# Four transformer stages on one core: the weight fold on column tiles, keys parked in fetch order, late weights as steps of ScalarE, the low-rank product on two row tiles

## What is computed

```python
x = layernorm(x + attn0(x))   # 16 heads of 8, causal; q and k are low rank: x @ a @ b
x = layernorm(x + ffn0(x))    # silu(x w1) * (x w2), gelu(h1), gelu(h2), w3; width 512
x = layernorm(x + attn1(x))   # 16 heads of 8, not causal, softmax / sqrt(128)
x = layernorm(x + ffn1(x))    # below

# ffn1: the token's best expert of 8 picks a low-rank term of rank 4
top1 = argmax(x @ gate.T + gate_b)
h    = relu(x @ wi.T + wi_b + (x @ A[top1].T) @ B[top1].T)
out  = h @ wo.T + wo_b
```

## Time and profile before

| | us |
|---|---|
| median of 3 runs | 928.54 (925.82 to 929.03) |
| the profiled execution | 927.51 |
| its span, first to last instruction | 925.70 |
| PE busy | 870.4 (94%) |
| DVE busy | 670.8 (72%) |
| ACT busy | 488.5 (53%) |
| POOL busy | 185.6 (20%) |
| DMA, mean over the span | 70 GB/s |

### The profile page before, as it was taken

One profiled execution on the slowest core, in us unless ns is written; L12 is line 12 of the kernel. 1 busy time (PEld: TensorE's weight loads), 2 busy tenths in 40 slices (PEclk: granted clock), 3 DMA queues, 4 the chain that ended last, 5 costly groups with the idle time before them and its releaser, 6 DMA issues.

```text
span 925.7 us, 19247 instructions
## 1 busy us (share of the span) xinstructions
PE 870.4 (94%) x7076; PEld 689.3 (74%) x7076; DVE 670.8 (72%) x2379; ACT 488.5 (53%) x951; POOL 185.6 (20%) x389
## 2 busy tenths in 40 slices
PE   5589899999999999999999999999999999999996
PEld 4358687876777876688777887778867888787855
DVE  5767658749998579964799659965899659654863
ACT  1143454376655545645547665646565665562372
POOL 2132221003400233002320034002320114010211
PEclk9879899999999999999999999999999999999999
DMA  7613031402322034301252023400442022002200
GB/s 243 205 47 104 20 98 53 126 13 60 105 71 77 1 93 129 87 2 37 68 145 76 2 70 113 116 10 1 118 115 71 7 75 65 13 8 63 81 15 12
DMA packets 49044, 65.17 MB, mean 70 GB/s; under 512 B 5624, under 2 KB 42744, under 8 KB 44248
## 3 DMA queue, kind: packets, MB, share of 16 engines
q1 hardware_dynamic: 46552, 58.02, 21.9%
q10 hardware_dynamic: 2400, 5.93, 1.9%
HBM read 48.46 MB, written 14.68 MB: 68 GB/s over the span
## 4 chain that ended last, share of the span: by engine, by line
PE 65%; DVE 12%; DMA 11%; issue 4%; ACT 4%; SPq 3%; POOL 1%; ACTq 0%; POOLq 0%; DVEq 0%
PE banks L1003 19%; PE banks L916 8%; PE banks L934 8%; DMA krow<-scratch 7%; PE banks L883 6%; PE banks L985 5%; PE banks L1052 4%; DVE top L704 3%; PE banks L838 2%; DMA scratch<-split 2%; DMA qrow<-tsplit 2%; SPq L439 1%; PE banks L874 1%; PE banks L1033 1%; PE banks L1034 1%
## 5 line engine op out<-in xcount | busy, mean ns | idle before, releaser
L575 ACT ACTIVATE prob<-banks 128x384 f32<-128x384 f32 (+1 forms) x512 | 247.0, 550 | 117.2 <-PE banks L916 97.4
L704 DVE TENSOR_REDUCE top<-banks 128x2 f32<-128x512 f32 (+1 forms) x280 | 176.0, 680 | 38.5 <-PE banks L883 27.9
L695 DVE CUSTOM_DVE_ANT_0 banks<-banks,above 128x128 f32<-128x128 f32 x448 | 145.5, 388 | 42.0 <-PE banks L883 29.6
L916 PE MATMUL banks<-qrow,krow 75*128 75x256 bf16 (+1 forms) x1024 | 155.6, 266 | 8.6 <-ACT prob L575 3.9
L883 PE MATMUL banks<-krow,qrow 72*128 72x256 bf16 x768 | 133.9, 277 | 9.2 <-DVE top L704 5.0
L916 PEld LDWEIGHTS banks<-qrow,krow 75*128 75x128 bf16 x1024 | 89.5, 100 | 47.0 <-ACT prob L575 11.2
L934 PE MATMUL banks<-prob,v 128*32 128x256 f32 (+1 forms) x2048 | 122.8, 367 | 0.7 <-POOL prob L515 0.6
L508 POOL TENSOR_TENSOR ln_rstd<-ln_var,minus_half 128x2 f32<-128x2 f32 x64 | 44.8, 703 | 380.6 <-DVE ln_var L764 380.3
L1003 PE MATMUL banks<-glu,wh 128*128 128x256 f32 x512 | 116.5, 381 | 1.0 <-ACT prob L575 1.0
L1003 PE MATMUL banks<-hid,wh 128*128 128x256 f32 x512 | 115.9, 380 | 0.0
L1003 PEld LDWEIGHTS banks<-glu,wh 128*128 128x128 f32 x512 | 94.9, 190 | 13.8 <-ACT prob L575 1.2
(11 more groups left out here) (100 smaller groups left out, 1164.1 us busy)
## 6 DMA issues: line engine op xcount, KB each, us to landing
qrow<-scratch SPq DMA_DIRECT2D x30, 576.0 KB
krow<-scratch SPq DMA_DIRECT2D x90, 192.0 KB
scratch<-split SPq DMA_DIRECT2D x96, 128.0 KB, 1.9
xt<-in_xt SPq DMA_DIRECT2D x16, 128.0 KB, 2.4
x<-in_x SPq DMA_DIRECT2D x16, 128.0 KB, 2.7
wh<-in_wh ACTq DMA_DIRECT2D x2, 1024.0 KB, 8.5
out<-xout SPq DMA_DIRECT2D x16, 128.0 KB, 2.0
qrow<-tsplit SPq DMA_DIRECT2D x90, 8.0 KB
```

Of the source, the lines that this page charges most:

```text
L575: nc.scalar.activation(prob[s][:, j % 2, g, 0:wide], banks[:, b, 0:wide], ACT.Exp, scale=1.0 / float(np.sqrt(np.float32(HD))) if s == A0 e ...
L695: done = nc.vector.tensor_tensor_reduce(out=bank[:, g * wide:(g + 1) * wide], in0=bank[:, g * wide:(g + 1) * wide], in1=above[:, 2 * P - w ...
L704: nc.vector.tensor_reduce(out=dst, in_=src, axis=AX, op=ALU.max, negate=True).then_inc(maxed[s], 1)
L916: done = nc.tensor.matmul(bank[:, kb * SEQ:(kb + 1) * SEQ - q0], krow[s][n % DEEP[s]][0:ROWSM, h, kb * P:(kb + 1) * P], qrow[s][n % DEEP[s ...
```

## The change

**The fold.** The factors change roles: 16 products with 16 columns of weights (`wqb`) and 128 moving columns (`wqa`), each on one of four column tiles, in two banks that DVE has set to zero; DVE copies each bank to `turned` (a piece of `glu`), PE transposes four times, and DVE copies into `wq` in four pieces.

**Parking.** The keys get a DRAM tensor of their own, `kscratch`, as feature, part, head, token, so a fetch of 24 rows reads one row after the other. `park` issues two DMAs per part. `fetch` and `key_rows` read it; of chunk 0's six key DMAs one is now SP's.

**Late weights.** ACT's loads beyond the first four become three steps of its order. The fills of `krow` for three of four buffers move to POOL, with a semaphore `rowed`; that of `wlb` is gone.

**The low-rank product.** The picked rows are written twice (columns 0 to 31 and 32 to 63 of `low`), `wlb` is loaded twice, and `expert` is one step with two banks: four products with `wi`, then four with `wlb`, of 32 rows each, alternating between two row tiles and two banks. The wait for `lowt` stands between them.

`SEQUENCE` and `BANK_TABLE` are new throughout. The diff's core:

```diff
-            scratch = {s: [nc.dram_tensor(..., [2, PARTS, P, TOK], BF16, ...)
+            scratch = {s: [nc.dram_tensor(..., [PARTS, P, TOK], BF16, ...)
+            kscratch = {s: [nc.dram_tensor(..., [HD, PARTS, HEADS, TOK], BF16, ...)
...
 def park(s, n, g):
-    sp.dma_start(scratch[s][n % 2][:, i].rearrange("a p t -> p a t"), split[s][:, i]).then_inc(parked[s][n % 2], DMA)
+    sp.dma_start(scratch[s][n % 2][i], split[s][:, i, 0]).then_inc(parked[s][n % 2], DMA)
+    sp.dma_start(kscratch[s][n % 2][:, i], split[s][:, i, 1]).then_inc(parked[s][n % 2], DMA)
 def fetch(s, n):
+    if n < 2 and (s, n) != (A0, 0):
+        sp.wait_ge(rowed, 3)
...
-    scratch[s][n % 2][1].rearrange("j (c h) t -> c j h t", c=HD)[:, :, heads].rearrange("c j h t -> c j (h t)")
+    kscratch[s][n % 2].rearrange("c j h t -> (c j) h t")[:, heads].rearrange("r h t -> r (h t)")
...
 @block.scalar
-    act.dma_start(early[...], d_in["scales"]...)
-    act.dma_start(w12[:], d_in["w12"])
-    for dst, name in (wq1, wv1, wo1, wi, wgl, wlb, wout): act.dma_start(dst, d_in[name])
+    def late(s, n, k):   # k == 0: scales, w12; 1: wh twice, w3; 2: the eight others
...
 @block.tensor
-    for pair in range(HEADS // 2):
-        for side in range(2):
-            at = banks[:, 0, side * D:(side + 1) * D].rearrange("p (c h) -> p c h", h=HEADS)[:, :, 2 * pair:2 * pair + 2]
-            done = nc.tensor.matmul(at, wqa[:, pair, side, :], wqb[:, pair, side, :]..., start=True, stop=True)
+    for half in range(2):
+        for side in range(2):
+            for i in range(4):
+                pair = 4 * half + i
+                done = nc.tensor.matmul(banks[32 * i:32 * i + 2 * HD, half, side * D:(side + 1) * D], wqb[:, pair, side, :],
+                                        wqa[:, pair, side, :], start=True, stop=True, skip_group_check=True)
+        done.then_inc(folded, 1)
+    for half in range(2):
+        pe.wait_ge(kept, half + 1)
+        for side in range(2):
+            done = nc.tensor.transpose(banks[:, 2 + half, ...], turned[:, half, ...], ident[:])
...
-def expert(s, n, m, g):
-    if m == 0: pe.wait_ge(lora_done, 1 * n + 1)
-    for i in range(2):
-        nc.tensor.matmul(at, wi[:, cut], xt[F1][n % AHEAD][:], start=True, stop=False)
-        done = nc.tensor.matmul(at, wlb[:, cut], lowt[:], start=False, stop=True)
+def expert(s, n, ga, gb):
+    for pair, g in enumerate((ga, gb)):
+        for i in range(2):
+            nc.tensor.matmul(banks[:, g, i * TOK:(i + 1) * TOK], wi[:, m * P:(m + 1) * P], xt[F1][n % AHEAD][:], start=i == 0, stop=False, ...)
+    pe.wait_ge(lora_done, 1 * n + 1)
+    for i in range(2):
+        for pair, g in enumerate((ga, gb)):
+            m, tile = 2 * pair + i, slice(pair * ER, (pair + 1) * ER)
+            done = nc.tensor.matmul(banks[:, g, i * TOK:(i + 1) * TOK], wlb[tile, m * P:(m + 1) * P], lowt[tile], start=False, stop=True, ...)
```

More of the change, by code:

```diff
@@ L68 @@
 CAUSAL = 2
-BARE = ('load', 'scale', 'keys', 'resid', 'fetch', 'norm', 'store')
+BARE = ('load', 'late', 'scale', 'keys', 'resid', 'fetch', 'norm', 'store')
 KIND = {
     "a": ("qk", A0), "b": ("v", A0), "c": ("pass1", A0), "d": ("early", A0),
-    "e": ("pass2", A0), "f": ("maxima", A0), "g": ("values", A0), "h": ("outputs", A0),
+    "e": ("maxima", A0), "f": ("pass2", A0), "g": ("values", A0), "h": ("outputs", A0),
     "i": ("merge", A0), "j": ("project", A0), "k": ("turn", A0), "l": ("norm", A0),
@@ L80 @@
     "u": ("down", F0), "v": ("turn", F0), "w": ("scale", F0), "x": ("norm", F0),
[L81 to L86, removed]
+    "y": ("late", F0), "z": ("qk", A1), "A": ("v", A1), "B": ("pass1", A1),
+    "C": ("maxima", A1), "D": ("pass2", A1), "E": ("values", A1), "F": ("outputs", A1),
+    "G": ("merge", A1), "H": ("project", A1), "I": ("turn", A1), "J": ("early", A1),
+    "K": ("norm", A1), "L": ("osum", A1), "M": ("resid", A1), "N": ("fetch", A1),
+    "O": ("route", F1), "P": ("lora", F1), "Q": ("expert", F1), "R": ("down", F1),
+    "S": ("norm", F1), "T": ("resid", F1), "U": ("store", F1),
 }
@@ L97 @@
[L97 to L101, removed]
@@ L168, in parts_of @@
             "scale": [(k,) for k in range(4)],
+            "late": [(k,) for k in range(3)],
             "gated": [(m,) for m in range(PAIRS)],
-            "hidden": [(layer, m) for layer in range(2) for m in range(PAIRS)],
-            "expert": [(m,) for m in range(PAIRS)]}.get(name, [()])
+            "hidden": [(layer, m) for layer in range(2) for m in range(PAIRS)]}.get(name, [()])
 def sequence(engine):
@@ L193, in shared_banks @@
         elif step[0] not in BARE:
-            count = 2 if step[0] == "gated" else 1
+            count = 2 if step[0] in ("gated", "expert") else 1
             of[step] = [int(b) for b in BANK_TABLE[bank:bank + count]]
@@ L391, in build @@
         NWEIGHTS2 = 2 * DMA
-        NWEIGHTS = 7 * DMA
+        NWEIGHTS = 8 * DMA
         NSCALED = 5
@@ L813, in _ @@
         def _(pe):
[L815 to L817 removed]
+            pe.wait_ge(zeroed, 1)
+            for half in range(2):
+                if half == 0:
+                    pe.wait_ge(weights0, 2 * DMA)
+                else:
                     pe.wait_ge(weights0b, DMA)
                 for side in range(2):
[L820 to L826 removed]
+                    for i in range(4):
[3 more added lines that the diff above has]
+                done.then_inc(folded, 1)
+            pe.wait_ge(made, 2)
+            for half in range(2):
+                pe.wait_ge(kept, half + 1)
+                for side in range(2):
+                    done = nc.tensor.transpose(banks[:, 2 + half, side * D:(side + 1) * D], turned[:, half, side * D:(side + 1) * D], ident[:])
+                done.then_inc(unturned, 1)
+            pe.wait_ge(wready, 4)
             last = Last()
```

213 lines of the change are left out of this document (115 added, 98 removed).

## The result

| | before | the change |
|---|---|---|
| median of the runs | 927.18 us (4 runs, 919.10 to 929.03) | 960.49 us (4 runs, 958.39 to 964.12) |
| ratio, 95% interval | | 1.0381 [1.031, 1.0451] |
| profiled execution, span | 927.51, 925.7 us | 960.04, 958.0 us |
| granted clock of PE, mean | 0.981 | 0.951 |

I forecast 914.5 us, 906 to 926. The time is 34 us above that range.

The account below looks back on a forecast made before the run. PE's own work was taken to bound the kernel (busy 94% of the span). Gains of 7.7 + 1.0 + 1.0 + 2.5 + 1.8 = 14.0 us took 927.51 to 913.5, as a median 914.5 us; range 906 to 926.

Parts of the forecast that it names:

- Part 1: Low-rank product on two row tiles: 7.7 us gained over 14 chunks, plus 1.0 us at the end.
- Rival A: Low-rank product: the row tiles don't run side by side, giving 926 us; chance 0.13.
- Rival B: Merged expert step: PE runs out of free banks for 1.7 us a chunk, giving 941 us; chance 0.07.
- Part 4: PE's new step order: 1.8 us gained from fewer value runs; waits in the middle unchanged, 6 us either way.
- Part 2: Fold and start: first projection near 9.8 us, 3.2 us earlier; 2.5 us gained at the start, bounds 0 and 8.
- starts near 49 as before: Start: chunk 1's fetch is issued at 39 to 42 us after maxima ending about 37, so its start is unmoved.
- Rival C: Start: chunk 1's fetch sits behind the maxima, so only the product gains; 5.3 us less, 920 us; chance 0.17.
- Part 3: Parking and fetching keys' rows: 0.4 us more latency per park, 1 us gained per fetch, 1.0 us gained in the middle.
- beside PE's full middle this is hidden: Parking: the 0.4 us added latency per park costs nothing in the middle and is paid once at the start.
- My own sign of being wrong: Middle, 100 to 850 us: the forecast is wrong if PE's idle time, near 17 us, grows by over 6 us.
- an estimate of 1.3 us: Keys' fetch: gain if a transfer uses 12 DMA engines instead of 8; 1 us a fetch was taken.
- My 1.8 us for fewer runs of values: PE's step order: values stand in 95 runs instead of 104, at 0.2 us each.

Follow-up runs that it names:

- e1: The change in its own order, but keys parked and fetched as in the kernel before; 933.27 us, ratio 1.0029 to the kernel before.
- e17: The kernel before plus only the fold and late weights, low-rank products over 128 rows, old order and parking; 920.89 us, ratio 0.9952.
- e22: The kernel of e17 run once more, beside e21; 924.50 us, ratio 0.9959 to the kernel before.
- e7: The change with its two parking transfers per part, but keys' rows in the old layout; 952.11 us, ratio 1.0282 to the kernel before.
- e15: The change with keys' parking on its own semaphore, waited for only after the queries' fetch is issued; 933.37 us, ratio 1.0024.
- e5: The kernel before with only the change's new parking (two transfers per part, new keys' layout); 939.53 us, ratio 1.0116.
- e16: The kernel before with the new parking and a separate semaphore for the keys, as in e15; 928.12 us, ratio 1.0011.
- e21: e1 with the low-rank products over all 128 rows, as in the kernel before; 936.93 us, ratio 1.0070 to the kernel before.
- e3: The change with the step order and banks of the kernel before, the joined expert step at the second one's place; 967.60 us, ratio 1.0395.
- e4: e3 with keys parked and fetched as in the kernel before; 949.35 us, ratio 1.0229 to the kernel before.
- e9: e1 with SP's first steps (chunk 1's load and fetch) back in their old place; 931.04 us, ratio 1.0049 to the kernel before.

## Why the prediction was wrong

**Part 1, the product: right in kind.** The rows' 1.07 us a chunk was forecast, 1.13 came. I took 7.7 us gained. PE's own time fell by 10.6 against 128 rows, the time by 4, between kernels whose intervals overlap. Rival A (no pairing) is refuted by L1071. Rival B (the joined step stops PE for 1.7 us a chunk) isn't borne out, since no wait for it stands among PE's largest; a smaller cost of the joined step is not excluded (Part 4).

**Part 2, the start: the fold right, what follows it not.** 9.8 us forecast for the first projection, 9.47 measured. The sentence that chunk 1 "starts near 49 as before" failed by 4 us: the fetch was issued at 44.09, not at 39 to 42, because the maxima were late (42.0 and not 37), and I had missed that SP's load of chunk 1's x now stands behind the parking. The 0.4 us for parking was too small here as well: e1's start, with the old parking, is 2.8 us ahead at the first product and 2.5 at chunk 1's. Rival C was the nearer one for the start. In the old order the fold and the late weights gain 4 us (e17, e22); I had taken 2.5.

**Part 3, parking: this step failed, and it decides.** It said "0.4 us more latency per park", "beside PE's full middle this is hidden", and 1 us a fetch gained. Measured: 0.79 us lost and 0.32 gained. I added one more issue of 0.37 us; I did not see that the keys' transfer in the new layout is slow to issue (0.60; 0.43 in e7, with the old layout), nor that the count the fetch waits for is complete only with the receipt of the last transfer. Worse was "hidden". I had read a busy PE as slack. But 732.85 us busy of 750 says how much PE works, not how far ahead of need the transfers land, and an order fitted to one latency has little room for another (3.5% lost in the new order, 1.2% in that of before). Each chunk has such a chain in two stages, from projection to pass one, 32 in all and 30 from chunk 1 on. The queries' fetch goes out 0.87 us later on each than in e15. That this times 30 is 26 us, near the 27 that came back, is no proof of the path: not every fetch is waited for, and by the records 14 us of it are idle time and 13.5 slower work (below). In the order of before 0.89 us (e5 to e16) costs 1.05%, 10 us: there more than half is covered. My own sign of being wrong came true: the idle time between 100 and 850 us grew by 14 us, from 17.2 to 31.2. The bound could have been had from the earlier trace rows, which shows four chains late already: even my 0.4 us, on 30 chains, is 12 us, and I put none of it into the range.

The rule of the page "DMA: Bandwidth & Descriptors" of the Trainium skill that I weighed there, more engines on the keys' fetch, gave an estimate of 1.3 us. The trace gives 0.32, and each 8 KB packet took 0.538 us for 0.453; no row here shows how many engines a transfer used, so the rule itself is neither shown nor refuted.

**Part 4, the order: taken as free, and it isn't.** "I take no change, and 6 us either way" held for no run: e21 against e17 and e22, 1.0070 against 0.9956, is 10.5 us lost to the new order and the joined step together. Which of the two it is the runs don't separate; e3 and e4 were to, and their joined step was badly placed. My 1.8 us for fewer runs of values was not seen.

**A term that was missing: the clock.** I knew the two levels and priced only the last chunks by them. From the change to e15 PE's idle time falls by 14 us (75.8 to 61.8, the span less the busy time), and its busy time by another 13.5 (882.2 to 868.7), with 96 and 41 us at the lower clock. The second half is the clock's: PE's 7080 records stand in the same order in both traces, and the 6454 that ran at the upper level in both take the same time, to 0.01 us in sum; 382 that ran at the lower level in the change alone take 18.5 us more, 78 that did so in e15 alone 5.5 less. That the falls of the clock come from the waits for keys' rows is only in part shown: four of the six in the middle stand right behind one, but e9, with the old parking, had 64 us at the lower level too.

My rival with a slower end (B) had the wrong mechanism. The range had no width for the one edit that lengthens a chain for which PE had been seen to wait.

## What to carry to other kernels

A transfer that is split in two under one semaphore makes its reader wait for the slower receipt; give each its own count, and wait for each where its data is used. Where a profile shows even a few short waits for a kind of transfer, count the chains of that kind and price an added latency on each, with the clock that may fall behind the gap, before calling it hidden. Products of another tiling mode should stand together: 0.2 us a change is small once and was some 20 us when it came 128 times.

## What the runs showed of the hardware

- A DRAM write of 64 KB in the order of the fetch took 0.60 us to issue where the plain order took 0.36 (L430, L429).
- With keys' rows read one after the other, some 11 packets were under way at once for 9, and each 8 KB packet took 0.538 us for 0.453: the fetch of 1.18 MB fell only from 8.73 to 8.41 us.
- f32 products on two row tiles, here writing to two banks, ran in pairs: 8 records in 1.13 us.
- A change from f32 products over 128 rows to such over 32 rows cost 0.19 us of PE's time (0.408 for 0.216), the way back 0.20, or 0.10 to a bf16 score product.
- In the middle of the change's run, six gaps of 0.95 to 2.14 us in PE's work were followed by stretches of 3.4 to 17.1 us at 1.2 GHz. Most gaps of that length were not: one of 2.09 us at 157 us and one of 1.53 at 416 were followed by none.
